# A Swin block on one Trainium2 core: the MLP's transposing transfers issued from SyncE instead of ScalarE, the output store in two halves

## What is computed

```python
x1 = shortcut + out                                   # out: the attention, projected
h = _ln(x1, norm2_g, norm2_b)
h = jax.nn.gelu(h @ fc1_w + fc1_b, approximate=False) # 48 -> 192
h = h @ fc2_w + fc2_b                                 # 192 -> 48
return x1 + h
```

## Time and profile before

| | us |
|---|---|
| median of 3 runs | 1094.67 (1093.88 to 1095.0) |
| the profiled execution, its time | 1094.25 |
| the profiled execution, its span | 1092.5 |
| PE busy in the span | 946.4 (87%) |
| DVE busy | 891.7 (82%) |
| ACT busy | 773.7 (71%) |
| POOL busy | 751.6 (69%) |

### The profile page before, as it was taken

The page is one execution under the profiler, slowest core; times in us unless marked ns, Lnnn a source line. Parts: engine busy times, 40 slices in busy tenths (PEclk is TensorE's granted clock), DMA queues, the critical chain, the costliest instruction groups (busy, mean ns, idle before and its releaser), DMA issues. The chain is left out here.

```text
span 1092.5 us, 45511 instructions
## 1 busy us (share of the span) xinstructions
PE 946.4 (87%) x16004; PEld 750.9 (69%) x16004; DVE 891.7 (82%) x2021; ACT 773.7 (71%) x1733; POOL 751.6 (69%) x971
## 2 busy tenths in 40 slices
PE   0489999999999999999999999999983688888887
PEld 0268887888788878887888788887873355554555
DVE  5678888888888888888888888898975677777776
ACT  0368888888888888888888888888863444444544
POOL 6258888888888888888888888888865444444441
PEclk9999999999999999999999999999996899999999
DMA  1022222222222222222222222232220343444444
GB/s 54 22 72 74 67 74 72 64 65 75 73 62 65 74 72 63 65 76 73 61 65 75 73 62 66 75 75 64 64 62 1 69 96 91 97 96 92 98 93 96
DMA packets 139237, 77.32 MB, mean 71 GB/s; under 512 B 105923, under 2 KB 138980, under 8 KB 139190
## 3 DMA queue, kind: packets, MB, share of 16 engines
q1 hardware_dynamic: 86966, 63.83, 22.3%
q10 hardware_dynamic: 52224, 12.85, 6.1%
HBM read 10.48 MB, written 9.63 MB: 18 GB/s over the span
## 5 line engine op out<-in xcount | busy, mean ns | idle before, releaser
L405 POOL TENSOR_TENSOR pl<-p 113x294 f16<-113x294 f32 x512 | 347.7, 690 | 46.6 <-ACT p L476 34.9
L476 ACT ACTIVATE p<-banks 113x294 f32<-113x294 f32 x512 | 214.8, 420 | 48.1 <-PE banks L655 41.0
L639 PE MATMUL banks<-Qh,KAg 128*128 128x147 f16 x2048 | 217.8, 228 | 0.0
L801 DVE TENSOR_REDUCE rowmax<-banks 113x12 f32<-113x588 f32 x256 | 192.5, 752 | 10.2 <-PE banks L622 8.3
L639 PEld LDWEIGHTS banks<-Qh,KAg 128*128 128x128 f16 x2048 | 166.5, 97 | 30.9
L1115 DVE TENSOR_TENSOR gl<-gel 128x448 f16<-128x448 f32 (+1 forms) x192 | 123.9, 647 | 64.2 <-ACT gel L1015 64.1
L655 PE MATMUL banks<-Vb,p 113*128 113x36 f16 x3072 | 175.3, 180 | 0.9 <-POOL pl L405 0.9
L608 PE MATMUL banks<-bs_h,idt 113*128 113x294 f16 x512 | 146.4, 293 | 31.3 <-DVE QAg L795 25.4
L655 PE MATMUL banks<-Vb,pl 113*128 113x36 f16 x1536 | 162.7, 180 | 0.0
L655 PEld LDWEIGHTS banks<-Vb,p 113*128 113x128 bf16 x3072 | 156.1, 97 | 1.1 <-POOL pl L405 1.1
L245 POOL TENSOR_TENSOR rstd<-var,mhalf 112x7 f32<-112x7 f32 x64 | 95.3, 1489 | 83.7 <-ACT var L240 83.7
(11 more groups left out here) (140 smaller groups left out, 2664.8 us busy)
## 6 DMA issues: line engine op xcount, KB each, us to landing
Qh<-QAB SPq DMA_DIRECT2D x192, 98.0 KB, 2.2
Vb<-Vn SPq DMA_DIRECT2D x256, 54.0 KB, 2.1
xres<-in_x SPq DMA_DIRECT2D x64, 147.0 KB, 2.2
KAh<-KA SPq DMA_DIRECT2D x192, 49.0 KB, 1.9
out_y<-ybuf SPq DMA_DIRECT2D x64, 147.0 KB, 2.1
Qh<-mT SPq DMA_DIRECT2D x128, 4.6 KB, 2.2
hT<-xtok ACTq DMA_TRANSPOSE x32, 2.8
hT<-htok ACTq DMA_TRANSPOSE x32, 2.7
```

The lines of the kernel that those rows point to most:

```text
L405: nc.gpsimd.tensor_tensor(pl[p % 4][:, :, :, 0:N].rearrange("p a w n -> p (a w) n"), p32[p % 4][:, :, :, 0:N].rearrange("p a w n -> p (a w ...
L476: nc.scalar.activation(p32[p % 4][:, :, :, 0:N].rearrange("p a w n -> p w a n"), src, ACT.Exp, scale=1.0 / SB).then_inc(s_exp, 1)
L639: i = nc.tensor.matmul(bank[:, w * COLS:(w + 1) * COLS], KAg[upar][:, 2 * p + w, :, :].rearrange("p g n -> p (g n)"), Qh[upar][:, level, : ...
L801: nc.vector.tensor_reduce(rowmax[:, 2 * p:2 * p + 4, :].rearrange("p (k w) a -> p k (w a)", k=2), sc[0:AP_, :, 0:2 * COLS].rearrange("p k ...
```

## The change

The transposing transfer hT(t+2) is issued by SP instead of ACT, and ACT's wait for the low part ahead of the third GELU piece goes with it. SP's step now waits for the output of unit t-1, issues the store of the first half of its columns, waits for the low part of unit t+2, issues the store of the second half, and issues the transposing transfer. In step 0, which has no store, SP waits for fc1 of unit 0 instead. As there are two transfers for each output, the counts on the store's semaphores double.

```diff
         def _(sp):
             def step(t, par):
+                def store(half):
+                    cols = slice(half * CH * C // 2, (half + 1) * CH * C // 2)
+                    sp.dma_start(out[bass.ds(t - 1, 1), :, cols].rearrange("u p n -> p (u n)"),
+                                 ybuf[1 - par][:, cols]).then_inc(s_store[1 - par], 16)
+
                 if exists(t - 1):
                     sp.wait_ge(s_yo, done(t - 1))
-                    sp.dma_start(out[bass.ds(t - 1, 1), :, :].rearrange("u p n -> p (u n)"),
-                                 ybuf[1 - par][:, :]).then_inc(s_store[1 - par], 16)
+                    store(0)
+                elif exists(t):
+                    sp.wait_ge(s_h, 3 * done(t))
+                if exists(t + 2):
+                    sp.wait_ge(s_mlo, done(t + 2))
+                if exists(t - 1):
+                    store(1)
+                if exists(t + 2):
+                    sp.dma_start_transpose(hT[par][:, :, :], htok[par][:, :, :].rearrange("p c n -> p (c n)"))\
+                      .then_inc(s_hT[par], 16)
             mlp_phase(sp, step)
             for par in range(2):
-                sp.wait_ge(s_store[par], 16 * UNITS // 2)
+                sp.wait_ge(s_store[par], 32 * UNITS // 2)
...
                 if exists(t):
                     gelu(1)
-                if exists(t + 2):
-                    act.wait_ge(s_mlo, done(t + 2))
                 if exists(t):
                     gelu(2)
-                if exists(t + 2):
-                    act.dma_start_transpose(hT[par][:, :, :], htok[par][:, :, :].rearrange("p c n -> p (c n)"))\
-                      .then_inc(s_hT[par], 16)
...
                 if exists(t - 1):
                     dve.wait_ge(s_y, done(t - 1))
-                    wait(dve, s_store[1 - par], 8 * (t - 1 - (1 - par)))
+                    wait(dve, s_store[1 - par], 16 * (t - 1 - (1 - par)))
```

## The result

| | before | after |
|---|---|---|
| median, us | 1094.84 (4 runs, 1093.88 to 1096.41) | 1125.45 (4 runs, 1122.16 to 1128.61) |
| span of the profiled execution, us | 1092.5 | 1126.8 |

The ratio is 1.0282, with a 95% interval of 1.026 to 1.0304: 30.6 us slower by the medians. The prediction said 1102, slower by 7.5, with a range that ended at 1114. The direction was right, the size was not.

A forecast was written before the change was run, and what follows sets the result against it. Bound: a loop of waits through ScalarE's transposing-transfer issue, 7.40 us per two steps. A new 7.60 us loop through SyncE adds 6.6 us over 30 double steps, the start 0.9, the tail at most 0.3: 1102 us, range 1096 to 1110.

The forecast's parts named there:

- What bounded the kernel before: MLP: ScalarE's transposing-transfer issue, scaled high part, first GELU, then VectorE's GELU and token low parts; 7.40 us per two steps.
- The new loop: MLP over two steps: fc1, GELU, VectorE's low parts and output, SyncE's half stores, transposing transfer, fc1 again; 7.60 us.
- SyncE's part: From the output's end through both half-store issues to the transposing transfer's issue: 0.98 us, bounds 0.54 to 1.14.
- fc1 to G0: From fc1's start on TensorE to the first GELU on ScalarE: 0.58 us.
- S1 to Y: On VectorE, from the low part of the second GELU result to the output: 1.16 us.
- T to fc1: From the transposing transfer's issue to the fc1 that reads it: 2.87 us.
- S2 beside GpSimd: VectorE's low part of the third GELU result, slowed by GpSimd's multiplication: 0.74 us to the output instead of 0.54.
- Rival 3: Transposing transfer's packets queue behind stores on SyncE's queue: +0.5 us a double step, 1117 us; chance 0.13 with rival 4.
- The halves: The split store gains nothing and lies on the loop's path; one whole store would be 0.49 us shorter, 7.11.
- rival 4: TensorE falls to the lower clock behind longer waits: double step 8.0 us, +12 us; chance 0.13 with Rival 3.
- The price: Lower clock's cost: first fc1 matmul 0.56 us instead of 0.36, some 0.4 on the way to the first GELU.
- The signs that the prediction named: Transfer issued about 1.0 us after the output's end; fc1 and ScalarE's high part await its landing; output 3.75 after fc1's start.

The follow-up runs named there:

- one whole store: The changed kernel with the output stored whole again, one store and then the transposing transfer on SyncE: 1105.67 us, ratio 1.0105 to the kernel before.
- added matmuls: The changed kernel with four more matmuls a step on TensorE, ahead of its wait for the transposing transfer: 1109.97 us, ratio 1.0153 to the kernel before.
- half, T, half: The changed kernel with the transposing transfer issued between the two half stores: 1098.85 us, ratio 1.0049 to the kernel before.

## Where the prediction held and where it failed

- **What bounded the kernel before** was right: ScalarE's issue of T in a loop with H, G0, S0 and L. With half of fc1's matmuls taken away the pace of before stayed (7.40 at the upper level); with T off ScalarE and not behind Y the step fell from 3.70 to 3.10.
- **The new loop** was right in every member, and 0.19 short: 7.79 instead of 7.60. SyncE's part is where it was short: from the first half's issue to T's it took 0.93 (963.35 to 964.28) where 0.81 stood, since the second half's wait and address take 0.24 and a further 0.05 lies ahead of T. From Y's start to the first issue it took 0.69 where 0.66 stood. The other terms came out within 0.01: fc1 to G0 0.59 (forecast 0.58), S1 to Y 1.17 (1.16; 961.49 to 962.66 in VectorE's timeline), T to fc1 2.88 (2.87). The issue of a half is 0.32, as taken: it does not go with the bytes. Over 60 steps the 0.19, with the unrolled steps, is 6.3 us.
- **S2 beside GpSimd** was mis-told without harm: S1 and S2 ran undisturbed at 1.04 together, and GpSimd's multiplication, which started second, took 1.31 to 1.38 instead of 0.84. The sum is the same, because 0.13 came instead between S2's end and Y, part of it on VectorE's sequencer. That it came out is luck.

```profile
961.49 1.04 DVE L1123 TENSOR_TENSOR gl<-gel 128x336 f16<-128x336 f32 x2
961.82 1.32 POOL L1014 TENSOR_TENSOR mxn<-xc,refined 112x336 f32<-112x336 f32 x1 [1.97 <-DVE htok L1130]
```

- **Rival 3** (T behind the stores) did not come about in the changed kernel: T landed in 2.75, and the halves' data ended 0.2 before T's began. With one whole store T came 0.25 later, half of the rival's 0.5, and by overlap: T's data began no later.
- **The halves**: 0.57 a double step where 0.49 stood. One whole store and then T was to give 7.11 and gave 7.51; that whole and half stores leave T's landing alone was wrong.
- **The step that failed is rival 4, the lower clock.** With rival 3 it had a chance of 0.13. It was counted small because "the waits in the new loop would be below 2 us", and no row showed that waits below 2 us leave the clock up: waits of 1.3 to 1.5 us, and one of 1.89, preceded the seven falls. The prediction's own numbers had it. Two steps of 7.60 and 2 x 2.96 of work leave 1.7 us of waiting; before, 7.40 left 1.5, but in two parts: the trace of before lists 49 waits ahead of fc2 between 880 and 1060 us, the longest 0.8. What was not seen is that two loops side by side need not stay evenly spaced, so that nearly all of the waiting can fall into one step. The waits of before and after in that stretch (us in total, times, longest):

```profile
PE banks L1065 <- DVE gl L1115: 32.9, 49, 0.8
...
PE banks L1060 <- DMA hT<-htok: 22.2, 21, 1.5
PE banks L1060 <- DMA hT<-xtok: 9.6, 17, 1.0
```

TensorE waited 32.9 us before and 31.8 after, and 28.7 with one whole store, where the longest wait was 1.3 and the clock fell too. That is 0.7, 0.7 and 0.6 a step: the sum hardly differs, the length of the single waits does.

The price was wrong too. It stood as 0.4 a double step on the way to G0; in fact at the lower level fc1 and fc2 fill TensorE and take 5.07 a step instead of 3.90, and the clock was low for stretches, not all the time. Of the 30.05 us, 60 steps at 7.79 / 2 are 233.7 and explain 12.9; the other 17.2 go with the lower level. The added matmuls gave back 13.7 of them; the 3.5 that they left lie at the start of the phase.

The signs that the prediction named were there: T issued 1.1 us after Y's end, fc1 and H released by the landing of hT, and Y's end 3.8 after fc1's start.

The sum once more, for the profiled execution: 7.5 forecast, 6.3 from a double step of 7.79, 17.2 from the clock, and 3.3 from both ends, of which 1.25 lie before the first fc1, where the program is the same (the profiled executions of all these kernels reach it between 851.1 and 855.2): 34.3. The median of the runs lies some 3 us lower, with granted clocks of 0.956 to 0.962 where the profiled one has 0.955.

## To carry to other kernels

Moving an issue to an idle queue also moves it behind whatever that queue's program waits for. Look for the last wait ahead of it and close the loop with that wait in it, because a wait that nobody cared about can become the pace. When a change adds waiting on TensorE, price the lower clock as well: add up the waiting of all steps of a loop, assume that it can fall into one of them, and take the pace at half speed from rows at that level. A cheap test is a few idle matmuls in the wait: here the time fell by 1.3%, and the part that they gave back was the clock's.

## What the runs showed of the hardware

- TensorE's clock fell in steady loops behind waits of 1.3 to 1.5 us (after), 1.23 to 1.31 (one whole store) and 1.20 and 1.50 (before, with less work). It stayed at 1.00 in the loops whose longest waits were 0.7 (added matmuls), 0.8 (before) or 1.0 (half, T, half, from 900 to 1075 us). Not every wait of 1.3 was followed by a fall: with one whole store three of them came in a row before it. Taking away 0.66 of its 2.96 us a step in the kernel before lowered it to between 0.72 and 0.83.
- A transposing transfer is issued in 1.21 to 1.23 us from SyncE in the changed kernel, and in 1.23 from ScalarE before; a store of 73.5 KB is issued in 0.32 there, as one of 147 KB. A store's landing goes with its size a little: 1.7 against 2.0 us.
- VectorE and GpSimd hold each other up, and whichever starts second takes longer: L 1.05 instead of 0.50 behind GpSimd's centring, GpSimd's multiplication 1.31 to 1.38 instead of 0.78 to 0.85 behind S1 and S2. The Trainium skill, "SBUF — State Buffer", section "SBUF: two separate sides", describes a port pair shared by VectorE and GpSimd as an exclusive lock: of a VectorE operation with two SBUF inputs and a GpSimd operation that reads SBUF, whichever starts first holds it for the whole instruction and the other fully blocks. The rows agree on who loses, in both directions; the time lost is 0.1 to 0.2 us less than what was left of the first operation (L: 0.56 lost, with 0.70 of the centring left).
